# Perceiver cross-attention on one core: six instead of four of 17 value groups as high and low parts, softmax sums divided anew between GpSimd and VectorE, reciprocals taken on two columns

## The reference, cut to what matters

```
k_full = concat([k_ctx, k]); v_full = concat([v_ctx, v])      # 4352 keys, 4 KV heads, each used by 4 of 16 heads
scores = einsum('blhd,bmhd->bhlm', q, k_full) / sqrt(128) + mask
probs  = softmax(scores, axis=-1)                              # max, exp, sum over 4352 keys
out    = einsum('bhlm,bmhd->blhd', probs, v_full) @ wo
```

## Time and profile before

| what | value |
|---|---|
| median of the runs shown | 983.13 us |
| the profiled execution | 983.72 us, its span 982.0 us |
| TensorE busy | 967.6 us, 99% |
| VectorE busy | 769.8 us, 78% |
| ScalarE busy | 619.6 us, 63% |
| GpSimd busy | 578.3 us, 59% |
| chain of waits, by engine | PE 81%, DVE 8%, POOL 5%, DMA 2%, issue 2%, ACT 1% |

### The profile page before, as it was taken

How to read it: one execution, slowest core, us unless ns; L and a number is a source line. 1 busy time by engine, 2 the same in 40 slices (tenths; PEclk the granted TensorE clock), 3 DMA queues, 4 the chain that set the end, 5 groups by cost and what they waited for, 6 DMA issues and landing times.

```text
span 982.0 us, 15915 instructions
## 1 busy us (share of the span) xinstructions
PE 967.6 (99%) x5727; PEld 854.2 (87%) x5727; DVE 769.8 (78%) x1167; ACT 619.6 (63%) x1058; POOL 578.3 (59%) x457
## 2 busy tenths in 40 slices
PE   9999999999999999999999999999999999999998
PEld 7888888888889999999999999978689988888887
DVE  6664778654988888888898898886798877777775
ACT  5444444335767777777777877762587666666663
POOL 3754555453298999999999999996001132222222
PEclk9999999999999999999999999999999999999999
DMA  8669867678503221141204033251800785555540
GB/s 295 196 222 334 278 206 247 193 238 301 190 1 102 81 82 34 43 140 53 61 2 156 30 116 110 76 182 44 343 2 1 286 303 195 193 182 183 186 157 22
DMA packets 72046, 148.93 MB, mean 152 GB/s; under 512 B 5889, under 2 KB 51361, under 8 KB 70433
## 3 DMA queue, kind: packets, MB, share of 16 engines
q1 hardware_dynamic: 71968, 147.92, 44.8%
HBM read 110.12 MB, written 37.78 MB: 151 GB/s over the span
## 4 chain that ended last, share of the span: by engine, by line
PE 81%; DVE 8%; POOL 5%; DMA 2%; issue 2%; ACT 1%; SPq 0%; POOLq 0%; DVEq 0%; ACTq 0%
PE bank L614 17%; PE bank L643 16%; PE bank L522 11%; PE bank L540 9%; PE bank L944 9%; PE bank L946 5%; POOL running L1947 2%; PE bank L637 1%; PE bank L752 1%; PE bank L639 1%; PE bank L641 1%; POOL k_rs L1911 1%; DVE turned L1074 1%; DVE w_hl L1039 1%; PE bank L549 1%
## 5 line engine op out<-in xcount | busy, mean ns | idle before, releaser
L614 PE MATMUL bank<-qT_hi,kT 128*128 128x256 f32 (+1 forms) x1088 | 295.5, 343 | 1.5 <-ACT weights L1646 1.5
L643 PE MATMUL bank<-weights,vN 128*128 128x256 f32 (+1 forms) x832 | 239.8, 375 | 0.0
L1947 POOL TENSOR_TENSOR running<-running,weights 128x1024 f32<-128x1024 f32 x90 | 214.9, 2388 | 6.5
L614 PEld LDWEIGHTS bank<-qT_hi,kT 128*128 128x128 f32 x1088 | 196.2, 189 | 18.9 <-ACT weights L1646 1.8
L1646 ACT COPY weights<-bank 128x512 f32<-128x512 f32 (+1 forms) x272 | 153.9, 582 | 85.0 <-DVE running L1099 44.1
L1112 DVE TENSOR_TENSOR running<-bank,running 128x512 f32<-128x512 f32 x196 | 134.8, 688 | 27.6 <-ACT weights L1646 21.5
L1138 DVE TENSOR_TENSOR weights<-weights,bank 128x1024 f32<-128x1024 f32 x128 | 154.6, 1211 | 1.8 <-PE bank L670 1.8
L614 PE MATMUL bank<-qT_lo,kT 128*128 128x256 f32 (+1 forms) x544 | 153.2, 282 | 0.0
L1650 ACT ACTIVATE weights<-weights 128x1024 f32<-128x1024 f32 x144 | 144.8, 1008 | 4.5 <-DVE weights L1138 3.7
L540 PE MATMUL bank<-w_ctx_hi,ctx_hl 128*128 128x512 f32 x512 | 144.4, 394 | 1.5 <-ACT w_ctx_hi L1607 0.9
L944 PE MATMUL bank<-fT_parts,e_hl 128*128 128x512 f32 x392 | 139.9, 394 | 0.0
(11 more groups left out here) (265 smaller groups left out, 1813.2 us busy)
## 6 DMA issues: line engine op xcount, KB each, us to landing
e_raw<-in_experts SPq DMA_DIRECT2D x51, 768.0 KB, 4.4
k_spill<-k_stage SPq DMA_DIRECT2D x16, 1024.0 KB, 5.7
kT<-k_spill SPq DMA_DIRECT2D x15, 1024.0 KB, 5.2
v_spill<-v_stage SPq DMA_DIRECT2D x16, 512.0 KB, 6.6
vN<-v_spill SPq DMA_DIRECT2D x16, 512.0 KB, 3.5
ctx_raw<-in_ctx SPq DMA_DIRECT2D x15, 512.0 KB, 5.5
w_raw<-in_w_qkv SPq DMA_DIRECT2D x6, 1024.0 KB, 5.8
wo_chunk<-in_wo SPq DMA_DIRECT2D x32, 128.0 KB, 3.8
```

Of the source, the lines that this page charges most:

```text
L614: done = e.matmul(dst, kT[:, w, kt * P:(kt + 1) * P], qT[a][:, h, q0:L], start=m == 0, stop=m == 2)
L643: done = e.matmul(dst[:, q0:L], vN[:, kt, :], weights[:, cols], start=kt == 0, stop=kt == KTILES - 1)
L1947: e.tensor_tensor(run_sum[:, :, :], quad(h, 0) if j == 1 else run_sum[:, :, :], quad(h, j), ALU.add).then_inc(summed, 1)
```

## The change

Six groups instead of four are split, (2, 4, 6, 8, 10, 12), with a ring of three `pT` buffers instead of two. GpSimd no longer sums groups 12 to 15: VectorE does so in one reduction of 128 x 2048 elements (`sum_late_weights`), and GpSimd adds its result (`add_late_sum`). In heads 0 to 13 the reciprocal is taken on two columns: TensorE turns `both_sum` with two transposes, VectorE reduces them to two columns of sums and inverts those (`invert_sums`), TensorE spreads them with two transposes (`spread_sum`), and ScalarE copies the result to SBUF (`copy_inverse`). The last heads keep the old way. The `vL` tiles move to where `w_xb` and a part of `w_xa` are loaded, so those loads are issued later. The diff, with the changed semaphore counts left out:

```diff
-FINISH_AT = (10, 2)
+FINISH_AT = (11, 2)
...
-SUMS = NG // 2 + 3
+SUMS = 10
+LATE_SUMS, LATE_AT, ADD_LATE_AT = 12, 12, 1
+TURNED_HEADS, INVERT_AT, SPREAD_SUM_AT = NH - 2, 6, 9
...
-SPLITS = (3, 6, 9, 12)
-RING = 2
+SPLITS = (2, 4, 6, 8, 10, 12)
+RING = 3
...
@@ sum_weights (TensorE)
+                    if h < TURNED_HEADS:
+                        for qt in range(2):
+                            done = e.transpose(dst[:, qt * P:(qt + 1) * P], both_sum[:, qt * P:(qt + 1) * P], ident[:, :])
+                        done.then_inc(sum_all, 1)
+                        return
...
+            def spread_sum(h):
+                dst = bank[VALUE_BANKS[h % 2]][:, L:2 * L]
+                pe.wait_ge(ho, finished(h) + 2)
+                for qt in range(2):
+                    done = e.transpose(dst[:, qt * P:(qt + 1) * P], row_rden[:, qt:qt + 1].to_broadcast([P, P]), ident[:, :])
+                done.then_inc(sum_all, 1)
...
+            def sum_late_weights(h):
+                dve.wait_ge(expd, NQUAD * h + NQUAD - 1)
...
+                late = s_buf[h % 2][:, LATE_SUMS:SELF, :].rearrange("p g (t q) -> p q (g t)", t=2)
+                e.tensor_reduce(out=late_sum[:, :], in_=late, axis=AX, op=ALU.add).then_inc(own_summed, 1)
+
+            def invert_sums(h):
+                dve.wait_ge(sum_all, sums_read(h) + 1)
...
+                e.tensor_reduce(out=row_sum[:, :], in_=bank[VALUE_BANKS[h % 2]][:, L:2 * L].rearrange("p (q k) -> p q k", q=2),
+                                axis=AX, op=ALU.add).then_inc(ho, 1)
+                dve.wait_ge(ho, finished(h) + 1)
+                e.reciprocal(row_rden[:, :], row_sum[:, :]).then_inc(ho, 1)
...
@@ finish_head (VectorE)
-                e.reciprocal(rden_all[:, :], bank[VALUE_BANKS[z]][:, L:2 * L]).then_inc(ho, 1)
-                dve.wait_ge(ho, 2 * h + 1)
+                if h >= TURNED_HEADS:
+                    dve.wait_ge(sum_all, sums_read(h + 1))
+                    dve.wait_ge(ho, finished(h))
+                    e.reciprocal(rden_all[:, :], bank[VALUE_BANKS[z]][:, L:2 * L]).then_inc(ho, 1)
+                    dve.wait_ge(ho, finished(h) + 1)
+                else:
+                    dve.wait_ge(oT_hi, sums_read(h) + 1)
...
+            def copy_inverse(h):
+                act.wait_ge(sum_all, sums_read(h + 1))
+                e.copy(rden_all[:, :], bank[VALUE_BANKS[h % 2]][:, L:2 * L]).then_inc(oT_hi, 1)
...
@@ add_weights (GpSimd)
-                    fold_sums(h, SUMS * (h + 1) - 2)
-                elif g % 2 and j:
+                        e.tensor_tensor(both_sum[:, to:to + w], both_sum[:, to:to + w], here[:, lo:lo + w], ALU.add).then_inc(summed, 1)
+                elif g % 2 and j and g < LATE_SUMS:
...
+                elif g == LATE_SUMS + 1:
+                    fold_sums(h, SUMS * h + LATE_SUMS // 2 - 1)
+
+            def add_late_sum(h):
+                pool.wait_ge(own_summed, h + 1)
+                pool.wait_ge(summed, SUMS * (h + 1) - 1)
+                e.tensor_tensor(both_sum[:, :], both_sum[:, :], late_sum[:, :], ALU.add).then_inc(summed, 1)
...
@@ SyncE, after the loads of wo_hi
+            sp.wait_ge(pv, NG * H15 + SPLITS[3] + 1)
+            sp.wait_ge(w_xb_in, chunks_in + 16)
+            e.dma_start(w_xb[:, :, :], t["w_in"][:, :, 2 * DI:]).then_inc(w_xb_in, 16)
+            sp.wait_ge(pv, NG * H15 + SPLITS[-1] + 1)
+            e.dma_start(w_xa[:, 1:2, :], t["w_in"][:, 1:2, DI:2 * DI]).then_inc(w_xa_in, 16)
```

More of the change, by code:

```diff
@@ L144, in summed_at, with sums_read, finished @@
 def summed_at(h, g):
-    return SUMS * h + (SUMS - 2 if g == SELF else max(g // 2, 1))
+    return SUMS * h + (SUMS - 1 if g == SELF else max(g // 2, 1))
+def sums_read(h):
+    return h + min(h, TURNED_HEADS)
+def finished(h):
+    return 2 * h + min(h, TURNED_HEADS)
 def split_number(n):
@@ L284, in build_program @@
         w_xb = sp_.take("w_xb", [KD, 2 * NS + MH])
+        vL = [Region(nc, at_, 4 * BT * HD).take(f"vL{g}", [BT, HD], F32R) for g, at_ in zip(SPLITS, (
+            [region["spare"].base + sp_.used - 4 * KD * (2 * NS + MH) + 4 * BT * HD * i for i in range(4)]
+            + [region["v"].base + 4 * KD * DI + 2048 + 4 * DI + 4 * BT * HD * i for i in range(2)]))]
         m23 = region["s23"].again()
@@ L445, in wait_slot @@
                 port.wait_ge(pv, NG * (h - 2) + g + 1)
-                port.wait_ge(summed, summed_at(h - 2, g))
+                if LATE_SUMS <= g < SELF:
+                    port.wait_ge(own_summed, h - 1)
+                else:
+                    port.wait_ge(summed, summed_at(h - 2, g))
             elif h == 1:
@@ L721, in pe_program @@
                     sum_weights(h)
+                if h in range(TURNED_HEADS) and k == SPREAD_SUM_AT:
+                    spread_sum(h)
                 i = n - WO_MAIN if n < WO_MAIN + 4 else max(n - WO_MAIN - WO_PAUSE, 3)
@@ L1212, in dve_program @@
                     add_own_weights(n - 1)
+                h, k = divmod(n, NG)
+                if h in range(H15) and k == LATE_AT:
+                    sum_late_weights(h)
                 h, k = divmod(n - NG, NG)
+                if h in range(TURNED_HEADS) and k == INVERT_AT:
+                    invert_sums(h)
                 if h in range(H15) and k == FINISH_AT[h == H15 - 1]:
@@ L1676, in act_program @@
                 h, k = divmod(n - NG, NG)
+                if h in range(TURNED_HEADS) and k == SPREAD_SUM_AT + 1:
+                    copy_inverse(h)
                 if h in range(H15) and k == FINISH_AT[h == H15 - 1] + 1:
@@ L1961, in pool_program @@
                 add_weights(n)
+                h, k = divmod(n, NG)
+                if h in range(1, H15) and k == ADD_LATE_AT:
+                    add_late_sum(h - 1)
+                if h == H15 - 1 and k == SELF:
+                    add_late_sum(h)
                 if n == NG * H15 + OWN_SUMS - 1:
```

75 lines of the change are left out of this document (41 added, 34 removed).

## The result

The changed kernel takes 1029.32 us (median of 4 runs, 1028.3 to 1029.58) against 983.46 of the kernel before on the same chip (982.95 to 985.47): ratio 1.046, 95% interval 1.0442 to 1.0479. The forecast was 1007 us, with a range of 990 to 1017: the direction was right, but the loss of 46 us is nearly twice the forecast 24. The profiled execution has a span of 1026.6 us (982.0 before).

A forecast was written before the change was run, and what follows sets the result against it. TensorE was taken to bound the kernel, with helpers within 5 to 11%. 13 heads x 1.92 us = 25.0, less 1.0 at the ends, gives +24.0: span 982.0 to 1006.0, median 1007 us; range 990 to 1017.

The forecast's parts named there:

- TensorE stands still for 1.47 us at group 8: Each middle head: group 8's low part, behind ScalarE's SELF copy, is ready at s + 10.69, wanted at s + 9.22.
- a delay of 2.13 by group 12: Each middle head: GpSimd gives low parts every 3.66 us, so group 12 starts at s + 18.01 instead of s + 15.88.
- net 1.92 a head: Heads 1 to 13: 2.24 us of delay less 0.32 saved by two more split groups, 25.0 us in all.
- A head takes 28.7 us: Sign of a right forecast in the changed trace: a head takes 28.7 us instead of 26.8.
- The late sum takes 2.4 us: VectorE's reduction of 2048 elements, scaled from reductions of 512 and 256 elements at 1.13 ns an element: 2.4 us.
- its 0.65 more fit: VectorE's late sum replaces a 1.75 us reciprocal; the 0.65 us more fit into 0.84 us idle ahead of SELF.
- The bounds, 2.3 to 2.8: VectorE's late sum: 2.3 us scaled without a fixed part, 2.8 as four times the 512-element reduction.
- Third rival: Late sum costs 4.9 us, twice its estimate; VectorE reaches SELF 1.9 us late a head: 1031 us, chance 0.04.
- The ends, together -1.0: Heads 0, 14 and 15: -0.8 in head 0, 0.16 saved in head 14, about 0 from there into head 15.
- Head 0's gain of 0.8: Head 0, paced by GpSimd: group 12 starts at 281.4 against 282.18, -0.8 us, bounds -1.5 and 0.
- The turned inverse costs nothing: VectorE's inversion of two columns at the step behind SELF fits its idle time: nothing, upper bound 0.3 a head.
- The clock stays: TensorE's granted clock stays 1.00; the rival that it falls behind its waits gives 1028 us, chance 0.02.

The follow-up runs named there:

- near_late: Changed kernel, but VectorE's late sum reads eight neighbours per result instead of eight elements 1 KB apart (sums of wrong elements): 1009.78 us.
- near_late_cast: Changed kernel with the late sum reading eight neighbours per result, and ScalarE's exponential and cast of group 8 ahead of its SELF copy: 985.62 us.
- three_cast: Changed kernel with ScalarE casting group 8 before copying SELF, VectorE summing only groups 13 to 15, GpSimd adding group 12: 988.04 us.
- no_late: Changed kernel with four split groups (3, 6, 9, 12) and no late sum on VectorE, GpSimd summing all groups: 984.63 us.

## Why the prediction was right or wrong, step by step

- *TensorE stands still for 1.47 us at group 8, a delay of 2.13 by group 12, net 1.92 a head*: right. The wait is 1.49 in the timeline and group 12 comes 18.01 behind group 2, 2.13 more than the 15.88 that the prediction gives TensorE alone. `near_late`, with the duration that was forecast, takes 1.88 more a head than the kernel before, and with ScalarE casting first (`near_late_cast`) 1.75 of them go.
- *A head takes 28.7 us*: right for a late sum of 2.3 us (`near_late`, 28.63), wrong for the one that the kernel has (29.85).
- *The late sum takes 2.4 us and its 0.65 more fit*: this step failed. It takes 3.90. The bounds, 2.3 to 2.8, were two ways of scaling one row that has two elements for a result, where the step costs nothing, so they bounded nothing. That it fits was right for 2.3 us, and nearly so for 2.94 (0.13 a head, `three_cast` against `near_late_cast`); 3.90 costs 1.22 a head, 15.9 us, and 3.0 in heads 0 and 1.
- *Third rival, "decides from about 3.1 us on", chance 0.04*: that a long late sum costs time was right, and so was the threshold as far as the runs tell: with ScalarE casting first, 2.94 costs 0.13 a head over 2.28 (27.01 against 26.88), and 3.90 costs 1.08. The chance was far too small, and the place was wrong. The rival adds the lateness to the wait for SELF; that wait stayed (3.24 us against 3.15), and what appeared is TensorE's wait for a bank directly behind the late sum, 0.8 us a head, which stands nowhere in the prediction. With 3.90 the rival's sum would be 3.90 - 1.75 - 0.84 - 0.45 = 0.86 a head; without the 0.45 that it credits, 1.31. Measured is 1.22, so the size agrees better than the mechanism does.
- *The ends, together -1.0*: they are +1.1 in `near_late` (-0.3 in heads 0 and 1, +1.9 in heads 14 and 15, -0.5 behind them). I had cost the last heads at 0; TensorE waits 2.21 us for a low part at 675.34 there, and 2.34 at 694.08 in the changed kernel. Head 0's gain of 0.8 came to 0.3.
- *The turned inverse costs nothing; four more `v_low` in the first stage nothing*: right for both (`no_late`; the rest of the kernel moves by -0.4).
- *The clock stays*: right for the profiled execution, 1.00. It is not so in each execution: in the one of `near_late` that was profiled, the wait of 2.21 us above is followed by 2 us at 0.50, the level of 1.2 GHz:

```profile
676.00:678.00 2.00, 2.00 (x9) 1.81 (x8) 0.88 (x3) 1.97 (x3) 2.00 (x2) 0.50 0.00 0
```

No cost of it can be told: this execution took 1009.27 us, and the two at a mean clock of 1.000 took 1009.56 and 1010.0.

With the forecast's duration the sum is +24.0 against the 25.5 us of span that `near_late` adds. The rest, 19 us, is one mis-sized instruction.

## What to carry to other kernels

Before a duration is scaled up from another row, compare how it reads memory, not only its size: here the same reduction takes 2.29 or 3.59 us by its step. When a helper is 89% busy and runs back to back, an instruction on it has a budget (here about 1.2 us more than the reciprocal it replaced), and what exceeds it in one piece is paid nearly in full in every round. The bill comes where the helper frees the next buffer, not necessarily where everybody already waits for it. And a cast that somebody waits for should not stand behind a copy that itself waits: that order alone was worth 24 to 28 us.

## What was not expected of the hardware

- The step's penalty is absent with two elements for a result and there with four: 0.69 us against 1.88 and 3.59 for 512, 1024 and 2048 elements at the same step of 1 KB, where 0.69 and 2.29 are the times of 512 and 2048 neighbours. The number of results was 256 each time, so elements for a result and elements in all are not told apart. A step of 1056 bytes is no remedy (3.81 us for 2048).
- VectorE's addition of 1024 columns with both operands in SBUF takes 1.23 us alone and 2.61 beside GpSimd's additions; the reduction takes 3.59 and 3.64, and in the kernel an instruction of the same size with one operand in PSUM 1.21, GpSimd at work or not (L1173). By these rows a late sum made of additions would hardly have been cheaper: its first addition of 1024 columns takes up to 2.61 and leaves 1024 columns to fold (an estimate, no run has it). The Trainium skill, "SBUF — State Buffer", section "Who interferes with whom", says that VectorE contends with GpSimd's reads where both its inputs lie in SBUF, and never with a reduction; the trace agrees on both (1.23 against 2.61, and 3.59 against 3.64).
